# Other places for the quantization units, and split weights kept in DRAM for the second batch

## The chip, the cores and the metric

The kernel runs on one core of one Trainium2 chip. The metric is the device time of one execution in microseconds (us); the median of three runs of the kernel before is 3158.2 us (3157.79 to 3158.3).

## The reference

One launch computes two transformer layers on x (2 batches x 512 rows x 1024), in float32:

```python
x = x + xattn(layernorm(x), ctx, ctx, mask, wq, wk, wv, wo)     # 32 query heads, 8 key/value heads, rotary, softmax
x = x + router(layernorm(x))    # softmax over 64 experts, top 8: flat * sum(w) + w @ expert_bias
x = x + fake_quant(layernorm(x)) @ fake_quant(ctx)              # 8-bit codes, product of codes
x = x + (silu(y @ dq1.T) * (y @ dq2.T)) @ dq3.T                 # y = layernorm(x); dq = nf4(w), hidden size 2752
```

nf4(w) quantizes each block of 64 weights: it divides by the block's largest magnitude, takes the nearest of 16 code values, and multiplies back. Context rows number 1024 per batch.

## The kernel before, in words

The program has three stages, one after the other, each with an instruction list per engine written out by hand as a loop over slots. An engine works in program order and waits on semaphores. Matrix products take each float32 operand as a high part (float32r) and a low part (the rest), and run three TensorE (PE) matmuls per tile: high by high, low by high, high by low (`split_matmul`, L130). So each operand needs a copy on ScalarE (ACT) for the high part and a subtraction on VectorE (DVE) or GpSimd (POOL) for the low one.

**Front** (`front_stage`): 128 tiles of 24 matmuls, keys (32), values (32 + 32 around the second batch's keys) and queries (64). ACT rounds a head's weights, POOL makes their low half two tiles ahead (L714), DVE and POOL rotate key and query tiles (L658, L659, L728, L731). **Attention** (`attention_stage`): 64 heads in 256 steps of scores, softmax, transposes and mixing. **Tail** (`tail_stage`): slots 0 to 127 project the heads on wo ("head" slots, 12 matmuls each, a ring of four heads loaded from DRAM, rounded by ACT at L1634, low half by DVE at L1736 or POOL at L1912); then the FFN. The router and the quantized product of each batch are a chain of small links, put into given slots by `Chain`: batch 0 in head slots 64 to 111, batch 1 in slots 128 to 175. Before it the 16 context tiles are turned into codes: ACT scales (L1639), POOL clips (L1916), DVE rounds to bfloat16 (L1751), SP stores.

**The FFN's items** (`Plan`): the hidden size is cut into 22 chunks. Items 0 to 7 take chunks 0 to 7 for batch 0 alone, while the chain of batch 1 runs; items 8 to 15 take the same eight chunks for batch 1; items 16 to 29 take chunks 8 to 21 for both batches. An item has two slots of 12 matmuls for each of its gates (gate and up, one or two batches); every second item also holds the "down" slots of the pair before. For every item the weights come from DRAM (`load_weight`, three loads of 512 KB), PE turns them in six turns of four transposes (`turn`, L2021), ACT copies the high part (`weight_high`) and DVE subtracts for the low part (`weight_low`) into the buffers `gu` and `dn`, which alternate by item.

**The nf4 units** (`Nf4`): the quantization of w1, w2 and w3 is cut into 65 units of 128 x 1024 weights, which fill DVE, ACT and POOL beside the other work. A unit has DVE's maximum by block (L212 and two short ones), POOL's normalization (L224), seven ramps on ACT (L241), each followed by a step on DVE (L262, then L265 six times), then a subtraction on DVE (L268), a sign (L245) and three folds (L250) on ACT, two last steps on DVE (L271, L273), and POOL's multiplication (L278); SP loads and stores it. `Spread` cuts a unit into 12 places and spreads these over slots by weights. The units are split 34 / 12 / 8 / 11 over front, attention, the head slots and the FFN from item 8 on. A unit of the FFN must be stored before `load_weight` of its chunk.

Of the kernel before, what the change touches and what calls it, by code (L numbers as in the profile page):

```python
# [26 lines left out]
P = 128  # L27
# [49 lines left out]
TINY = 1e-30  # L77
SIGNS = NP4 + len(FOLDS)
NS4 = NP4 + len(FOLDS) + 2
# [57 lines left out]
class Nf4:  # L137
# [89 lines left out]
    def above_scalar(self, act, n, s, steps, width=D):  # L227
# [3 lines left out]
        for j in steps:  # L231
            f = j - NP4 - 2
            if j < NP4:
# [9 lines left out]
            if f == 0:  # L243
                act.wait_ge(self.stepped.sem, n * ND4 + 2 * ND4 + NP4 + 1)
                act.activation(x, x, ACT.Sign, bias=self.sharp[:, SIGNS:SIGNS + 1]).then_inc(self.above_done.sem, 1)  # L245
            if f >= 0:
                scale, _, slope = FOLDS[f]
                if f:
                    act.wait_ge(self.above_done.sem, n * NA4 + NP4 + 1 + f)
                act.activation(fold, fold if f else self.val[:, s, w], ACT.Prelu, bias=self.sharp[:, NP4 + f:NP4 + f + 1],  # L250
                               scale=scale, alpha=slope).then_inc(self.above_done.sem, 1)
# [43 lines left out]
class Spread:  # L295
# [4 lines left out]
    def __init__(self, units, weights, lag=1, sync_lag=1, ahead=8):  # L300
        total = units * NS4
        edge, run, whole = [0], 0.0, float(sum(weights))
        for w in weights:
# [5 lines left out]
        self.steps, self.maxes, self.norms, self.finishes, self.loads, self.stores = (  # L309
            [[] for _ in range(slots)] for _ in range(6))  # L310
        where = {}
        for q in range(len(weights)):
            for k in range(edge[q], edge[q + 1]):
                self.steps[q].append(divmod(k, NS4))
                where[divmod(k, NS4)] = q
        for u in range(units):
            if u:
                assert where[u - 1, ahead] < where[u, 0] and (u < 2 or where[u - 2, NS4 - 1] < where[u - 1, ahead])
                self.maxes[where[u - 1, ahead]].append(u)
                self.norms[where[u - 1, ahead] + lag].append(u)  # L320
# [29 lines left out]
def front_stage(nc, ident, sharp, x, context, wq, wk, wv, tables, q_d, k_d, v_d, rows, units, handover):  # L350
# [4 lines left out]
    with ExitStack() as ctx:  # L355
# [132 lines left out]
        plan = Spread(len(units), [weight(kind, n) for kind, n, _ in ORDER])  # L488
# [140 lines left out]
        def _(dve):  # L629
# [44 lines left out]
            for q, (kind, n, half) in enumerate(ORDER):  # L674
# [28 lines left out]
                for u, j in plan.steps[q]:  # L703
                    nf.step_vector(dve, u, u % 2, [j], parts[u], units[u][2])
                    if j == 8 and u + 1 < len(units):
# [5 lines left out]
        def _(pool):  # L711
# [26 lines left out]
            for q in range(plan.slots):  # L738
                kind, n, half = ORDER[q] if q < len(ORDER) else ("end", 0, 0)
                if kind == "tile":  # L740
# [4 lines left out]
                    if n == 64:  # L745
                        pool.wait_ge(tab_q, 32)
                for u in plan.norms[q]:
                    nf.norm_gpsimd(pool, u, u % 2, units[u][2])
                for u in plan.finishes[q]:
                    nf.finish_gpsimd(pool, u, u % 2, units[u][2])  # L750
# [70 lines left out]
def attention_stage(nc, q_d, k_d, v_d, r_d, o_d, mask, ident, ho, old, sharp, units):  # L821
# [8 lines left out]
    with ExitStack() as ctx:  # L830
# [84 lines left out]
        plan = Spread(len(units), [n >= UNITS_FROM for n in range(ALL - 4)], lag=2, sync_lag=6)  # L915
# [181 lines left out]
        def _(dve):  # L1097
# [27 lines left out]
            def do_step(n):  # L1125
# [9 lines left out]
                for u, j in planned(plan.steps, n - 1):  # L1135
                    nf.step_vector(dve, u, u % 2, [j], u // 2)
                    if j == 8 and u + 1 < len(units):
# [61 lines left out]
class Plan:  # L1199
# [8 lines left out]
    def __init__(self):  # L1208
        self.slots = [("head", q // HQ, q % HQ) for q in range(self.FIRST)]
        self.turn_no, self.turn_slot, self.turns = {}, {}, {}  # L1210
        self.gate_no, self.a_no, self.h_until = {}, {}, {}
# [18 lines left out]

    def _turn(self, i, x, q):
        if i < self.NI:
# [940 lines left out]
```

## Time and profile before

| | us |
|---|---|
| median of 3 runs | 3158.2 |
| the profiled execution | 3158.93 |
| its span, first to last instruction | 3157.2 |
| PE busy in the span | 2954.9 (94%) |
| DVE busy | 2311.9 (73%) |
| ACT busy | 1919.0 (61%) |
| POOL busy | 1094.0 (35%) |

The front lasts to about 845 us, attention to 1812, the head slots to 2287; items 0 to 7 of the FFN end at 2497, items 8 to 15 at 2639. Busy times are sums over instructions; matmuls are pipelined and their ends modelled, so a busy PE is not PE at its peak. The granted clock of TensorE is 1.00 at full speed.

### The profile page before, as it was taken

How to read it: one execution, taken by the hardware profiler on the slowest of the kernel's cores; microseconds unless marked ns; L12 is line 12 of the kernel's file. 1: busy time of each engine (PE TensorE's matmuls, PEld its weight loads, DVE VectorE, ACT ScalarE, POOL GpSimd, SP SyncE). 2: the span in 40 equal slices, each digit the busy share in tenths (PEclk: the TensorE clock that was granted, in tenths of full speed). 3: DMA queues.
4: the chain of work that ended last, by engine and by line, in shares of the span. 5: the costliest groups of instructions: out<-in, count | busy, mean ns of one | idle time of the engine just before them, and what ended most of it. 6: DMA issues, size and time to landing. Idle time of an engine off the chain costs nothing. (4 is left out here: it accounts for less than half of the span.)

```text
span 3157.2 us, 39853 instructions
## 1 busy us (share of the span) xinstructions
PE 2954.9 (94%) x14326; PEld 2414.3 (76%) x14336; DVE 2311.9 (73%) x3394; ACT 1919.0 (61%) x2643; POOL 1094.0 (35%) x644
## 2 busy tenths in 40 slices
PE   7989899989799999999999978998999999999999
PEld 6767687767588888888888856776786788888887
DVE  5878788788588888888888748788456666666633
ACT  4676666666488888888888756655343344444411
POOL 4626428777623333333333246543300000000000
PEclk9999999999899999999999989999999999999999
DMA  5445344343332222222222187743421232222111
GB/s 181 143 151 169 120 136 134 114 137 127 125 109 83 79 94 84 78 94 81 88 101 73 55 301 261 242 166 132 169 67 61 85 96 87 74 72 67 60 37 57
DMA packets 231108, 362.18 MB, mean 115 GB/s; under 512 B 19456, under 2 KB 114688, under 8 KB 230912
## 3 DMA queue, kind: packets, MB, share of 16 engines
q1 hardware_dynamic: 230912, 359.63, 34.4%
q8 instruction: 115, 1.88, 0.2%
q14 instruction: 81, 0.66, 0.1%
HBM read 266.90 MB, written 92.67 MB: 114 GB/s over the span
## 5 line engine op out<-in xcount | busy, mean ns | idle before, releaser
L1108 DVE CUSTOM_DVE_ANT_0 at_sc<-at_s,at_mk 128x1024 f32<-128x1024 f32 x256 | 312.0, 1219 | 100.6 <-issue 98.2
L132 PE MATMUL fr_acc<-fr_xh,fr_wh 128*128 128x512 f32 x768 | 308.8, 402 | 57.6 <-POOL fr_wl L714 52.4
L241 ACT ACTIVATE fr_nf_above<-fr_nf_raw,sharp 128x1024 f32<-128x1024 f32 (+1 forms) x238 | 258.8, 1103 | 164.6 <-POOL fr_nf_raw L224 107.0
L1123 DVE TENSOR_TENSOR at_ptl<-at_t,at_pth 128x512 fp32r<-128x512 f32 x512 | 326.5, 679 | 30.6 <-ACT at_pth L1070 30.6
L1070 ACT ACTIVATE at_pth<-at_t 128x512 fp32r<-128x512 f32 x512 | 277.4, 595 | 112.0 <-PE at_t L1170 111.3
L1060 ACT ACTIVATE at_pr<-at_sc,at_low 128x1024 f32<-128x1024 f32 x256 | 295.7, 1155 | 36.0 <-DVE at_low L1108 30.6
L133 PE MATMUL fr_acc<-fr_xl,fr_wh 128*128 128x512 f32 x768 | 305.4, 398 | 0.0
L134 PE MATMUL fr_acc<-fr_xh,fr_wl 128*128 128x512 f32 x768 | 305.0, 397 | 0.0
L1170 PE MATMUL at_t<-ident,at_pr 128*128 128x128 f32 x2048 | 267.8, 273 | 12.2 <-DVE at_ptl L1123 11.2
L1170 PEld LDWEIGHTS at_t<-ident,at_pr 128*128 128x128 f32 x2048 | 236.3, 140 | 53.9 <-issue 19.3
L265 DVE SCALAR_TENSOR_TENSOR fr_nf_val<-fr_nf_above,fr_nf_val 128x1024 f32<-128x1024 f32 (+1 forms) x204 | 246.5, 1209 | 20.4 <-ACT fr_nf_above L241 3.2
L132 PE MATMUL tl_pa<-tl_ring_h 128*128 128x512 f32 x512 | 210.0, 410 | 40.9 <-POOL tl_ring_l L1912 16.1
L1912 POOL TENSOR_TENSOR tl_ring_l<-tl_ring,tl_ring_h 128x1024 fp32r<-128x1024 f32 x64 | 162.5, 2539 | 193.6 <-ACT tl_ring_h L1634 193.5
L132 PEld LDWEIGHTS fr_acc<-fr_xh,fr_wh 128*128 128x128 f32 x768 | 148.4, 193 | 99.3 <-issue 58.0
L132 PE MATMUL at_o<-at_pth,at_vh 128*128 128x512 f32 x512 | 221.9, 433 | 0.2 <-DVE at_ptl L1123 0.2
L132 PE MATMUL at_s<-at_kh,at_qh 128*128 128x512 f32 x512 | 201.8, 394 | 11.8 <-POOL at_ql L1004 11.8
L1652 ACT ACTIVATE tl_gu<-tl_pt 128x512 fp32r<-128x512 f32 x120 | 71.7, 597 | 226.5 <-PE tl_pt L2021 226.5
L1764 DVE TENSOR_TENSOR tl_gu<-tl_pt,tl_gu 128x512 fp32r<-128x512 f32 x120 | 82.6, 688 | 169.8 <-ACT tl_gu L1652 169.2
L133 PE MATMUL tl_pa<-tl_ring_l,tl_ring_h 128*128 128x512 f32 x512 | 203.9, 398 | 0.0
L134 PE MATMUL tl_pa<-tl_ring_h,tl_ring_l 128*128 128x512 f32 x512 | 203.6, 398 | 0.0
L134 PE MATMUL at_s<-at_kh,at_ql 128*128 128x512 f32 x512 | 201.9, 394 | 0.0
L134 PE MATMUL at_o<-at_pth,at_vl 128*128 128x512 f32 x512 | 201.1, 393 | 0.0
(224 smaller groups left out, 7842.6 us busy)
## 6 DMA issues: line engine op xcount, KB each, us to landing
tl_raw<-dq SPq DMA_DIRECT2D x87, 512.0 KB, 3.6
tl_ring<-o_d SPq DMA_DIRECT2D x128, 256.0 KB, 3.2
tl_ring<-in_L_xattn_wo SPq DMA_DIRECT2D x128, 256.0 KB, 3.9
fr_nf_raw<-in_L_ffn_w SPq DMA_DIRECT2D x33, 512.0 KB, 3.6
dq<-fr_nf_val SPq DMA_DIRECT2D x33, 512.0 KB, 3.6
fr_raw<-in_L_xattn_wq SPq DMA_DIRECT2D x32, 512.0 KB, 4.5
q_d<-fr_res SPq DMA_DIRECT2D x64, 256.0 KB, 2.3
rows<-q_d SPq DMA_DIRECT2D x64, 256.0 KB, 2.7
```

The source lines that it names most:

```text
L132: pe.matmul(out, w[0], x[0], start=start, stop=False)
L133: pe.matmul(out, w[0], x[1], start=False, stop=False)
L134: return pe.matmul(out, w[1], x[0], start=False, stop=stop)
L241: act.activation(self.ramps[j % 2][:, w], x, ACT.Relu, bias=self.sharp[:, j:j + 1], scale=SHARP).then_inc(self.above_done.sem, 1)
L265: dve.scalar_tensor_tensor(v, above, STEPS[j], v, ALU.min, ALU.add).then_inc(self.stepped.sem, 1)
L1060: act.activation(pr[:, n % 2], sc[:, n % 2], ACT.Exp, bias=low[:, n % 2:n % 2 + 1], scale=-1.0, accum_out=sums[:, h % 2, quarter:quarter + ...
L1070: act.activation(pt[0][:, h % 2, j * HALF:(j + 1) * HALF, (n % QT) * P:(n % QT + 1) * P], t_ps[:, j], ACT.Copy).then_inc(t_hi.sem, 1)
L1108: dve.tensor_tensor_reduce(sc[:, n % 2], s_ps[:, n % 2], mk[:, bb * QT + n % QT], -1.0, -NEG, ALU.add, ALU.min, low[:, n % 2:n % 2 + 1]).t ...
L1123: dve.tensor_tensor(pt[1][sl], t_ps[:, j], f32(pt[0][sl]), ALU.subtract).then_inc(t_lo.sem, 1)
L1170: last = pe.transpose(t_ps[:, j, c, :], pr[:, n % 2, k * P:(k + 1) * P], ident[:])
L1764: dve.tensor_tensor(lo, pt[:, no % 2], f32(hi), ALU.subtract).then_inc(w_lo, 1)
L1912: pool.tensor_tensor(ring_l[:, q % 4], ring[:, q % 4], f32(ring_h[:, q % 4]), ALU.subtract).then_inc(ring_lo_p, 1)
```

## The change

- The units are split 28 / 12 / 6 / 19 (`chunks, late_units` from 12, 8 to 9, 6).
- Within a unit the folds come before the sign and do not wait for the subtraction; a unit has 11 places instead of 12. DVE takes a unit's step when ACT is at the next one (`late`), in the front and the tail. The next unit's maximum stands at place 5 (before: 8, in the tail 7). POOL takes finishes before normalizations. In the front SP loads and stores a unit one slot later. In the FFN a "down" slot has 0.3 of the weight of a gate slot.
- The context codes: ACT scales, rounds and codes (three passes), POOL clips between; DVE has no part. They begin at slot 5 instead of 3, and each tile is stored four slots after its scaling instead of two.
- DVE waits for the router's inputs at slot 62 instead of before its first low half; SP loads them at slot 40; the scales' loads, the first context tiles, and the loads of x come later and spread.
- In the chain, codes and product come one slot later, and the last normalization and turn too.
- Items 0 to 7 store their split weights to DRAM (`keep`, 24 stores of 1 MB on SP's queue). Items 8 to 15 load no raw weights and have no turns, copies or subtractions; POOL's queue loads the split weights back (`fetch`, 24 loads of 1 MB), and PE waits for these.

The core of the diff:

```diff
+AHEAD = 5
-NS4 = NP4 + len(FOLDS) + 2
+NS4 = NP4 + len(FOLDS) + 1
@@ Nf4.above_scalar
-            f = j - NP4 - 2
-            if j < NP4:
+            f = j - NP4
+            if f < 0:
...
+            elif f < len(FOLDS):
+                scale, _, slope = FOLDS[f]
+                if f:
+                    act.wait_ge(self.above_done.sem, n * NA4 + NP4 + f)
+                else:
+                    act.wait_ge(self.stepped.sem, n * ND4 + 2 * ND4 + NP4)
+                act.activation(fold, fold if f else self.val[:, s, w], ACT.Prelu, ...
+            else:
                 act.wait_ge(self.stepped.sem, n * ND4 + 2 * ND4 + NP4 + 1)
                 act.activation(x, x, ACT.Sign, bias=self.sharp[:, SIGNS:SIGNS + 1]).then_inc(self.above_done.sem, 1)
@@ Spread
                 where[divmod(k, NS4)] = q
+                if k:
+                    self.late[q].append(divmod(k - 1, NS4))
@@ front_stage
-        plan = Spread(len(units), [weight(kind, n) for kind, n, _ in ORDER])
+        plan = Spread(len(units), [weight(kind, n) for kind, n, _ in ORDER], lag=1, sync_lag=2)
...
-                for u, j in plan.steps[q]:
+                for u, j in plan.late[q]:
@@ Plan
+    def again(self, i):
+        return self.EARLY <= i < 2 * self.EARLY
     def _turn(self, i, x, q):
-        if i < self.NI:
+        if i < self.NI and not self.again(i):
@@ Plan._item
+        self.item_slot[i] = len(self.slots)
+        for j in range(2):
+            self._fetch(i + 1, j, self.item_slot[i] + 1)
+        self._fetch(i, 2, self.item_slot[i] + (1 if i % 2 else len(mine) - 2))
@@ Chain._batch
-        r, z, y = [6 + 3 * t for t in range(QT)], [27 + 3 * t for t in range(QT)], [43 + t for t in range(QT)]
+        r, z, y = [6 + 3 * t for t in range(QT)], [27 + 3 * t for t in range(QT)], [44 + t for t in range(QT)]
...
-                put("pe", z[t] + 2, "product", t, h)
+                put("pe", z[t] + 3, "product", t, h)
@@ tail_stage, SP
+            def keep(i, j):
+                sp.wait_ge(w_lo, plan.turn_no[i, 2 * j + 3 if j < 2 else 1] + 1)
+                sp.dma_start(split_d[i, j], f32(parts_of(i, j))).then_inc(kept[j][i % 2], 16)
...
+                for i, xx in plan.turns.get(q - 2, []):
+                    if xx in (1, 3, 5) and i < plan.EARLY:
+                        keep(i, {3: 0, 5: 1, 1: 2}[xx])
@@ tail_stage, ACT
+            def round_context(n):
+                act.wait_ge(ones_made, 1)
+                act.wait_ge(ctx_scaled, n + 1)
+                act.activation(rows[:, n % 2], rows[:, n % 2], ACT.Identity, bias=rounding[:, 0:1]).then_inc(ctx_rounded, 1)
+            def code_context(n):
+                act.wait_ge(ctx_clipped, n + 1)
...
+                if 2 <= i < plan.EARLY:
+                    act.wait_ge(kept[(xx - 2) // 2 if xx >= 2 else 2][i % 2], 16 * (i // 2))
@@ tail_stage, DVE
-            dve.wait_ge(ro_in, 48)
             low(1)
             for q in range(TOTAL + 2):
+                if q == plan.BASE[0] - 2:
+                    dve.wait_ge(ro_in, 48)
@@ tail_stage, POOL
+            def fetch(i, j):
+                pool.wait_ge(kept[j][i % 2], 16 * max((i - plan.EARLY) // 2 + 1, min(i, plan.EARLY) // 2))
+                if j < 2:
+                    pool.wait_ge(gated, plan.gate_no[i - 2, plan.halves(i - 2)[-1], 1] + 1)
+                else:
+                    pool.wait_ge(y_tiles, plan.y_base[i // 2])
+                pool.dma_start(parts_of(i, j), split_d[i - plan.EARLY, j]).then_inc(fetched[j][i % 2], 16)
@@ tail_stage, PE
+                    if plan.again(i):
+                        pe.wait_ge(fetched[u][i % 2], 16 * ((i - plan.EARLY) // 2 + 1))
+                    else:
+                        pe.wait_ge(w_lo, plan.turn_no[i, 2 * u + 3] + 1)
@@ build
-    chunks, late_units = 12, 8
+    chunks, late_units = 9, 6
```

## Rows read from the trace of the kernel before

**Rows 1.** Windows by stage: length, PE, PEld, DVE, ACT, POOL busy; clock; DMA; GB/s.

```profile
0.00:500.00 500.00, 439.25 (x1950) 359.04 (x1951) 386.01 (x429) 325.90 (x370) 246.95 (x162) 0.97 0.46 149
500.00:845.00 345.00, 307.17 (x1286) 247.97 (x1285) 272.25 (x290) 216.00 (x238) 259.76 (x163) 0.96 0.38 123
845.00:1812.00 967.00, 942.80 (x5147) 792.20 (x5147) 809.54 (x1572) 794.76 (x1318) 309.75 (x190) 0.99 0.26 88
1812.00:2007.00 195.00, 155.95 (x649) 124.02 (x647) 126.60 (x106) 117.80 (x115) 109.42 (x52) 0.91 0.80 276
2007.00:2287.00 280.00, 260.61 (x1187) 201.06 (x1192) 212.49 (x263) 149.30 (x167) 119.09 (x50) 0.97 0.49 166
2287.00:2497.30 210.30, 198.74 (x1020) 155.01 (x1025) 132.71 (x252) 73.68 (x118) 4.18 (x4) 0.98 0.21 63
2497.30:2639.20 141.90, 141.87 (x710) 117.17 (x709) 91.69 (x126) 65.94 (x91) 11.44 (x6) 1.00 0.34 104
2639.20:3157.20 518.00, 508.55 (x2387) 417.81 (x2385) 280.65 (x362) 175.68 (x228) 33.37 (x19) 1.00 0.20 62
```

**Rows 2.** Waits of PE, 0 to 845 us: total, times, longest.

```profile
PE fr_acc L132 <- POOL fr_wl L714: 52.4, 21, 7.3
PE fr_acc L764 <- DVE rows L670: 15.1, 1, 15.1
```

**Rows 3.** Timeline of PE around one turn (start, length, instruction).

```profile
2468.16 0.39 PE L134 MATMUL tl_pa<-tl_yT,tl_gu 128*128 128x512 f32 x1
2468.39 0.60 PE L2021 MATMUL tl_pt<-ident,tl_raw 128*128 128x128 f32 x4
...
2469.06 0.39 PE L133 MATMUL tl_pa<-tl_yT,tl_gu 128*128 128x512 f32 x1
...
2471.34 0.39 PE L134 MATMUL tl_pa<-tl_yT,tl_gu 128*128 128x512 f32 x1
```

**Rows 4.** DVE's groups, 500 to 845 us: busy, mean ns, idle before.

```profile
L265 DVE SCALAR_TENSOR_TENSOR fr_nf_val<-fr_nf_above,fr_nf_val 128x1024 f32<-128x1024 f32 x78 | 95.6, 1225 | 6.5
L658 DVE TENSOR_TENSOR fr_tb<-fr_acc,fr_sin 64x512 f32<-64x512 f32 x53 | 36.7, 693 | 6.5 <-ACT fr_res L608 5.0
...
L262 DVE TENSOR_SCALAR fr_nf_val<-fr_nf_above 128x1024 f32<-128x1024 f32 x13 | 15.9, 1225 | 41.2 <-ACT fr_nf_above L241 41.1
```

**Rows 5.** POOL's groups, 500 to 845 us.

```profile
L731 POOL TENSOR_TENSOR fr_res<-fr_res,fr_tb 128x512 f32<-128x512 f32 x54 | 73.6, 1362 | 46.7 <-DVE fr_tb L659 45.8
...
L278 POOL TENSOR_TENSOR fr_nf_val<-fr_nf_val,fr_nf_am 128x1024 f32<-128x1024 f32 x13 | 24.8, 1910 | 0.0
```

**Rows 6.** DMA issues: KB each, median us to landing.

```profile
tl_ring<-in_L_xattn_wo SPq DMA_DIRECT2D x128, 256.0 KB, 3.9
...
tl_qb<-qb_d SPq DMA_DIRECT2D x2, 2048.0 KB, 9.7
...
at_mk<-in_mask_BxSxS_ff SPq DMA_DIRECT2D x1, 2048.0 KB, 13.2
```

**Rows 7.** The chain of waits, 1820 to 1845 us: start, length, what.

```profile
1826.72 13.47 DMA tl_two<-in_L_ffn_router_bias
```

**Rows 8.** Timeline of PE at the tail's start, idle time in brackets.

```profile
1825.11 0.80 PE L132 MATMUL tl_pa<-tl_ring_h 128*128 128x512 f32 x1 [12.18 <-POOL tl_ring_l L1912]
...
1841.56 0.79 PE L132 MATMUL tl_pa<-tl_ring_h 128*128 128x512 f32 x1 [11.27 <-DVE tl_ring_l L1736]
```

**Rows 9.** DVE's groups, 1840 to 2040 us.

```profile
L1751 DVE TENSOR_SCALAR tl_codes<-tl_rows 128x1024 bf16<-128x1024 f32 x16 | 27.0, 1686 | 6.7 <-POOL tl_rows L1916 6.7
...
L262 DVE TENSOR_SCALAR tl_nf<-tl_above 128x1024 f32<-128x1024 f32 x5 | 11.7, 2331 | 0.0
```

**Rows 10.** ACT's groups, 1840 to 2040 us.

```profile
L1634 ACT ACTIVATE tl_ring_h<-tl_ring 128x1024 fp32r<-128x1024 f32 x63 | 65.9, 1051 | 38.0 <-DMA tl_ring<-in_L_xattn_wo 20.4 <-PE tl_pa L134 17.3
...
L1639 ACT ACTIVATE tl_rows<-tl_rows,tl_two 128x1024 f32<-128x1024 f32 x16 | 19.7, 1230 | 0.0
```

**Rows 11.** Waits of PE, 2007 to 2287 us.

```profile
PE tl_pc L2060 <- DVE tl_two L1846: 8.6, 3, 4.2
```

More of the change, by code:

```diff
@@ L295, with __init__ @@
 class Spread:
-    def __init__(self, units, weights, lag=1, sync_lag=1, ahead=8):
+    def __init__(self, units, weights, lag=1, sync_lag=1, ahead=AHEAD, norm_lag=1):
         total = units * NS4
@@ L308, in __init__ @@
         self.units, self.slots = units, slots
-        self.steps, self.maxes, self.norms, self.finishes, self.loads, self.stores = (
-            [[] for _ in range(slots)] for _ in range(6))
+        self.steps, self.late, self.maxes, self.norms, self.finishes, self.loads, self.stores = (
+            [[] for _ in range(slots)] for _ in range(7))
         where = {}
@@ L315, in __init__ @@
                 where[divmod(k, NS4)] = q
+                if k:
+                    self.late[q].append(divmod(k - 1, NS4))
+        self.late[where[divmod(total - 1, NS4)] + 1].append(divmod(total - 1, NS4))
         for u in range(units):
@@ L319, in __init__ @@
                 self.maxes[where[u - 1, ahead]].append(u)
-                self.norms[where[u - 1, ahead] + lag].append(u)
+                self.norms[where[u - 1, ahead] + norm_lag].append(u)
             end = where[u, NS4 - 1]
@@ L914, in attention_stage @@
         nf = Nf4(tools, sharp)
-        plan = Spread(len(units), [n >= UNITS_FROM for n in range(ALL - 4)], lag=2, sync_lag=6)
+        plan = Spread(len(units), [n >= UNITS_FROM for n in range(ALL - 4)], lag=2, sync_lag=6, norm_lag=2)
         def planned(table, n):
@@ L1136, in do_step @@
                     nf.step_vector(dve, u, u % 2, [j], u // 2)
-                    if j == 8 and u + 1 < len(units):
+                    if j == AHEAD and u + 1 < len(units):
                         nf.max_vector(dve, u + 1, (u + 1) % 2, (u + 1) // 2)
@@ L1371, in due, with tail_stage @@
         return self.at[engine].get(q, [])
-def tail_stage(nc, o_d, wo, x, context, scales, router_w, router_b, expert_b, dq, dq3, qb_d, ident, ident_bf, sharp,
+def tail_stage(nc, o_d, wo, x, context, scales, router_w, router_b, expert_b, dq, dq3, qb_d, split_d, ident, ident_bf, sharp,
                o_units, f_units, chunk_unit, out):
@@ L1465, in tail_stage @@
         raw_in = [sem(f"raw_in{j}") for j in range(3)]
+        kept, fetched = [[[sem(f"{n}{j}{s}") for s in range(2)] for j in range(3)] for n in ("kept", "fetched")]
         zeroed, out_stored = sem("zeroed"), sem("out_stored")
@@ L1640, in scale_context @@
                                scale=kq[:, 1:2]).then_inc(ctx_scaled, 1)
+            def round_context(n):
[4 more added lines that the diff above has]
+                act.wait_ge(ctx_clipped, n + 1)
+                if n >= 2:
+                    act.wait_ge(ctx_out[n % 2], 16 * (n // 2))
+                act.activation(codes[:, n % 2], rows[:, n % 2], ACT.Identity, bias=rounding[:, 1:2]).then_inc(ctx_coded, 1)
             def weight_high(i, xx):
```

155 lines of the change are left out of this document (87 added, 68 removed).

## The prediction

> **What bounds the kernel now.** I read the busy time by stage first, then TensorE's (PE's) waits stage by stage, then the rows of the engine it waits for. Most stages are TensorE's own: attention (845 to 1812 us) has PE busy 942.8 of 967 us, the FFN from item 8 on 141.87 of 141.9 and 508.55 of 518 [rows 1]. PE loses time in two places. In the front (0 to 845) it is idle 500 - 439.25 = 60.8 and 345 - 307.17 = 37.8 us, and mean clocks of 0.97 and 0.96 cost about 0.03 x 439 + 0.04 x 307 = 25 us more [rows 1]. In the tail's projection (1812 to 2287) it is idle 39.0 and 19.4 us [rows 1]. In the front the largest wait is for POOL's low half of a head's weights, 52.4 us in 21 times; the largest single one is 15.1 us for DVE's normalized row [rows 2]. Both engines work in program order, so either wait is the lag of a queue filled with quantization units. In the query part (500 to 845) DVE handled 53 rotated tiles, 6.5 us each, where 24 matmuls at 0.228 us need 5.47 (ten spacings from 2469.06 to 2471.34 [rows 3]). DVE was busy 272.25 us [rows 1]; the rotations take 53 x 2 x 0.693 = 73 [rows 4], so the units take 199, or 14.7 each (78 whole L265 steps, 6 to a unit, and half a unit: 13.5 units). It also waited 41.2 us at L262 [rows 4], which makes 91% before smaller waits. POOL was busy 259.76 of 345 us [rows 1].
>
> **The change, part by part.** The sum is made against the profiled execution (3158.93 us, span 3157.2, so 1.7 us outside the span); the median shown is 3158.2, 0.7 lower, and I take the sum off the median.
>
> *Units 34/12/8/11 to 28/12/6/19.* Six units leave the front, two leave the projection, and eight join the FFN. In the query part DVE drops to 199 x 28/34 = 164 + 73 = 237 us per 53 tiles, 4.5 us a tile against 5.47; POOL loses 6/34 of its unit time (13.5 units x 2 x 1.91 = 52 us [rows 5]), 260 to 251, or 4.7 a tile. Both then fit under PE. Also, DVE now takes a step when ScalarE (ACT) is already at the next one, so the wait at L262 should mostly go; the subtraction and first fold no longer wait for each other; and a unit has 11 places instead of 12. What is late next is POOL: 2 x 1.36 us of its 4.7 are rotations [rows 5], and it waits for DVE's last step at each unit. The load of the next raw unit is issued one slot later as well, nearer to its reduction. I take 5.85 us a tile, between 5.47 and 6.5: 64 tiles x 0.65 = 42 us. Before 500 us I take 14 of the idle time, most of the 15.1 us wait. Front: -56; bounds -20 (POOL merely takes DVE's place) and -100 (all but the start-up's share of the 124 lost).
>
> *Eight more units in the FFN.* 8 x 14.7 = 118 us of DVE, beside PE. From 2639 us on DVE is busy 280.65 of 518 and ACT 175.68 [rows 1]. By the planner 1.57 unit steps fall on each gate slot in place of about 0.8, which is 1.57 x 14.7/11 = 2.1 us of a 2.73 us slot; with products, low halves and additions an item of 12 slots needs some 31 us of DVE under 35 of PE. Each unit still has 8 or more slots between its store and its use. I take +5 for adds that come late (a down tile needs the addition two tiles before); bounds 0 and +27, which is 7% of the 390 us in which units run, if DVE waits as it did in the front.
>
> *Kept weights.* For items 8 to 15, 8 x 6 = 48 turns of four transposes go from PE, with 48 copies on ACT and 48 subtractions on DVE, both off PE's path. A turn costs PE 0.444 us: from the matmul at 2468.16 to the second one after the turn, at 2469.06, is 0.90, where two plain spacings are 0.456 [rows 3]. 48 x 0.444 = 21.3. As a check: 528 matmuls x 0.228 = 120.4 us, and the stage takes 141.9 [rows 1]. All of it is on the path: -21. It adds 24 stores of 1 MB on SP's queue in items 0 to 7, each behind the loads of raw weights and ahead of the unit stores. SP waits there for DVE's low half; queued behind are the next raw loads, needed an item later. 24 MB over 210 us is 114 GB/s on top of 63, under the 276 that the projection carries for 195 us [rows 1]; ACT's copy two items later waits for a store that had an item's time. Cost 0; up to +15 if ACT stands at it, since the gates' activations queue behind. It also adds 24 loads of 1 MB on POOL's queue. Each waits for the gates of the item two before; behind it on POOL stand the clip, the unit's finish and its normalization, with slots to spare. No POOL-issued DMA is in this trace. The nearest rows are SP's: 2 MB landed in 9.7 and in 13.2 us [rows 6], so 4.9 to 6.6 per MB. An even item after an odd one gives 4 x 2.73 = 10.9 us for its first MB, so a load at either rate lands in time. With 1 MB for each of six units the traffic is 30 MB in some 125 us, 240 GB/s, also under 276. I take 0 (nearest the 9.7 us row, which is a load into SBUF amid other traffic); bounds 0 and 24 x 6.6 = 158 us against 120: +38.
>
> *Start of the tail.* DVE's first low half no longer waits for the router's bias: that transfer is 13.47 us of the chain [rows 7], and PE waited 11.27 us for the low half at 1841.56 [rows 8]. Next late are the ring's own loads. -12, with part of what the 0.91 mean clock of that stretch costs [rows 1]; bounds -8 and -15.
>
> *Context codes on ACT.* DVE loses 16 x 1.686 = 27.0 us [rows 9]. ACT gets two more passes for each of 16 tiles, one tile in 3 slots: 3 x 1.05 + 3 x 1.23 [rows 10] + 3 x 0.68 unit steps of about 1.1 = 9.1 us per 3 slots, where PE needs 8.2. So ACT bounds slots 5 to 53, at 16 x 0.9 = 14 us over PE. But PE now has 39.0 - 12.2 (before its first matmul [rows 8]) - 11.3 = 15.5 us of waits left in that stretch, mostly DVE's lag; one takes the other's place. 0; bounds -12 and +15. The loads of X, now spread, and scales later: 0, they relieve a queue at 276 GB/s.
>
> *Chain one slot later.* Codes, products and the last turn move by a slot. PE's 8.6 us of waits for L1846 [rows 11] and part of the other 11 idle us in that stretch go, with DVE lighter by a quarter of its units: -12; bounds -3 and -20. In items 0 to 7 the same gains about 3 and loses about 3: the last turn now stands right before the first gate of item 8, and its copy and subtraction must pass. 0.
>
> Sum: -56 + 5 - 21 - 12 + 0 - 12 + 0 = -96, so 3158.2 - 96 = 3062.
>
> **The rivals.** *POOL or DVE stays the bound* (23%): the front gains 20 instead of 56 and the FFN loses 15 instead of 5: 3062 + 36 + 10 = 3108. For it: POOL's 4.7 us a tile and its order; against: its 46.7 us of idle time at L731 [rows 5], nearly all of it for DVE. *The front becomes PE's* (10%): -95 in place of -56, 3023. For it: DVE falls to 82% of a tile.
>
> *The kept weights come too late from POOL's queue, slower than before* (6%): PE stands in items 8 to 15 for 24 loads. Decided at (120 + 96)/24 = 9.0 us per MB; above that the gain is spent. At four times a single 256 KB load's 3.9 us [rows 6], 15.6 per MB if POOL's queue carried only one small piece at a time, items 8 to 15 would take 374 us: 3062 + 254 = 3316. Against it: the 2 MB rows. For it: the rows show DVE and POOL holding each other up. The same kind of L262 takes 1.225 us in the front [rows 4] and 2.331 in the projection [rows 9], where POOL reads much of the time.
> The Trainium skill ("SBUF — State Buffer", section "SBUF: two separate sides") states that a DMA issued from GpSimd gets its descriptors from GpSimd's own cores, and that these are shut out while VectorE runs an instruction that takes their shared port pair, so that the transfer looks blocked. By that rule a load would start up to one such instruction late, 2.3 us by the row; three even items have 10.9 - 6.6 = 4.3 us to spare, so it costs nothing here unless it strikes many times in one load. The rows agree on the contention; none shows it on a DMA.
>
> *Nothing measurable* (4%): the front's gain missing and the FFN's DVE cost at its bound: -21 - 12 - 12 + 27 + 15 = -3.
>
> **How the numbers follow.** The forecast case, 3035 to 3095, has 57%. Low end 3015: the PE-bound front (3023) with some of the context stretch's -12. High end 3130: the POOL-bound case with 22 of the +38 for late loads. Runs of the kernel before differ by 0.5 us, so 0.2%, 6.3 us, is about what can be told from no change. Faster 57 + 23 + 10 = 90%, same 4%, slower 6%.
>
> **What would show it.** Front: the wait for L714's half falls from 52 to under 25 us, and attention begins near 790 to 800. Tail start: no wait of 11 us before the second head. Items 8 to 15: no transposes, and 120 to 125 us from the first gate to item 16; a wait of PE for a DMA into the weights there means the loads are late. FFN: DVE at about 85% of the stretch with units, PE above 97%. Wrong would be a front above 835 us, PE waits over 20 us in items 8 to 15, or a projection stretch longer than now.

## The result, and the profile after

The changed kernel takes 3132.5 us (median of 4 runs, 3126.09 to 3139.28) against 3158.25: 0.9912 of the time before, 95% interval 0.9900 to 0.9923, a gain of 26 us where 96 were forecast. Its profiled execution is the fastest of its four: 3126.09 us, 32.8 under that of before. The stages below sum to this number.

The windows by stage of the changed kernel (columns as in [rows 1]; the front now ends at 754 us, attention at 1729):

```profile
0.00:500.00 500.00, 476.47 (x2155) 394.48 (x2156) 379.28 (x423) 315.02 (x365) 275.79 (x180) 0.99 0.47 154
500.00:753.90 253.90, 252.58 (x1111) 207.65 (x1109) 199.99 (x222) 156.72 (x177) 216.47 (x137) 1.00 0.42 134
753.90:1728.90 975.00, 938.66 (x5121) 786.26 (x5120) 813.26 (x1567) 795.65 (x1317) 309.10 (x185) 0.99 0.26 87
1728.90:1918.50 189.60, 157.75 (x644) 126.10 (x645) 93.06 (x77) 138.37 (x137) 104.90 (x53) 0.91 0.77 267
1918.50:2206.00 287.50, 263.29 (x1193) 201.71 (x1191) 205.54 (x249) 137.26 (x155) 113.30 (x48) 0.96 0.51 173
2206.00:2413.60 207.60, 194.20 (x997) 150.58 (x997) 129.24 (x247) 70.09 (x112) 7.26 (x8) 0.99 0.52 188
2413.60:2549.50 135.90, 128.19 (x545) 104.43 (x545) 95.49 (x105) 65.94 (x69) 35.44 (x30) 0.95 0.57 197
2549.50:3121.00 571.50, 526.45 (x2387) 427.34 (x2384) 366.63 (x443) 247.91 (x297) 63.27 (x32) 0.97 0.20 66
```

PE is now busy 252.6 of 253.9 us in the query part: that part of the front is now limited by PE alone. In the last window PE is idle 45 us at a mean clock of 0.97, where it was idle 9.5 at 1.00 [rows 1].

For a comparison by stage I take the starts of fixed matmuls in the timelines of PE: the first score matmul and the last output matmul of attention, the first matmuls of head slots 5 and 53, and the first gates of items 0 (slot 128), 8, 16 and 27 (the 2nd column is a start, the others are lengths, in us).

| kernel | first score | attention | to slot 5 | slots 5-53 | slots 53-128 | items 0-7 | items 8-15 | items 16-26 |
|---|---|---|---|---|---|---|---|---|
| before | 863.5 | 949.0 | 42.6 | 152.3 | 279.7 | 210.2 | 141.9 | 396.7 |
| after | 765.0 | 963.5 | 28.0 | 162.1 | 287.5 | 207.5 | 135.9 | 453.6 |
| difference | -98.5 | +14.5 | -14.6 | +9.8 | +7.8 | -2.7 | -6.0 | +56.9 |

From item 27 on both kernels take 114.5 us to the start of the last tile. (The expectations below say "items 16 to 29" for the last column.) So the front alone gave what was forecast for the whole, and 89 us were lost again behind it: 14.5 in attention, 17.6 in the head slots and 57 in the FFN. Items 8 to 15 gained 6 where the kept weights were to give 21.

How far can such lengths be read? Among the profiled executions below, a stage that runs the same code still varies: the front by 5 us, attention by 5, slots 53 to 128 by 7, items 0 to 7 by 4, items 8 to 15 by 3, and slots 5 to 53 and items 16 to 26 by under 1. The changed kernel's 287.5 and 207.5 us in slots 53 to 128 and items 0 to 7 are at the short end of this; its 135.9 us in items 8 to 15 is the longest (132.6 and 132.8 in two other kernels with that code).

The 57 us of items 16 to 26 are not idle time alone. PE is idle 43.2 us there, against 4.2 before, and its busy time for the same matmuls grew from 392.5 to 410.4 us, at a mean granted clock of 0.96 against 1.00. So about 39 us are waits and 18 go with the lower clock.

PE's waits in the changed kernel (total, times, longest), first in the front, then from slot 128 to the end; and for items 16 to 26 alone, before and after:

```profile
PE fr_acc L770 <- DMA rows<-in_ctx: 9.1, 3, 6.5
PE fr_acc L133 <- POOL fr_wl L720: 5.9, 3, 4.6
...
PE fr_acc L770 <- DVE rows L676: 3.0, 2, 2.6
```

```profile
PE tl_pa L133 <- DVE tl_X L1834: 44.6, 16, 6.6
```

```profile
PE tl_pa L132 <- DVE tl_X L1776: 4.2, 5, 1.3
```

```profile
PE tl_pa L133 <- DVE tl_X L1834: 34.9, 11, 6.6
```

The 52.4 us for POOL's low half and the 15.1 us for the row [rows 2] are nearly gone from the front. DVE's rotations and POOL's, 500 to 754 us (busy, mean ns, idle before):

```profile
L664 DVE TENSOR_TENSOR fr_tb<-fr_acc,fr_sin 64x512 f32<-64x512 f32 x47 | 32.6, 693 | 42.2 <-ACT fr_res L614 41.9
```

```profile
L737 POOL TENSOR_TENSOR fr_res<-fr_res,fr_tb 128x512 f32<-128x512 f32 x47 | 65.7, 1397 | 11.7 <-DVE fr_tb L665 9.5
```

DVE, which had waited 41.2 us inside its units [rows 4], now waits 42.2 at the rotations, for ACT's copy of the next tile, while PE is idle 1.3 us in all: DVE no longer holds PE up there. POOL's wait for DVE, 45.8 us before [rows 5], is 9.5. In the FFN one wait has come up: a "down" matmul stands until DVE has added the tile that holds its PSUM buffer. DVE's timeline ahead of one such wait, and PE's and POOL's there (start, length, instruction, idle time before):

```profile
2628.66 1.22 DVE L268 SCALAR_TENSOR_TENSOR tl_two<-tl_two 128x1024 f32<-128x1024 f32 x1
2629.80 1.21 DVE L213 TENSOR_REDUCE tl_am<-tl_two 128x16 f32<-128x1024 f32 x1
...
2631.68 2.88 DVE L268 SCALAR_TENSOR_TENSOR tl_two<-tl_two 128x1024 f32<-128x1024 f32 x1 [0.18 <-issue]
2634.60 1.23 DVE L271 TENSOR_TENSOR tl_two<-tl_two 128x1024 f32<-128x1024 f32 x1
2635.74 1.28 DVE L1834 TENSOR_TENSOR tl_X<-tl_pa,tl_X 128x512 f32<-128x512 f32 x2
```

```profile
2636.48 0.80 PE L133 MATMUL tl_pa<-tl_dn,tl_hT 128*128 128x512 f32 x1 [5.45 <-DVE tl_X L1834]
```

```profile
2631.59 1.90 POOL L225 TENSOR_TENSOR tl_two<-tl_two,tl_am 128x1024 f32<-128x1024 f32 x1 [11.96 <-DVE tl_am L220]
```

For 7 us DVE does nothing but unit work: a step, the next unit's maximum, a step that takes 2.88 us instead of 1.22 while POOL normalizes beside it, and a subtraction. The addition that PE needs is queued behind. DVE is not full (325.2 of the 453.5 us of items 16 to 26); its work comes in lumps. In the longest wait, 6.6 us, DVE itself stands idle first, for ACT's sign (L254), with the addition behind the unit's last steps:

```profile
2960.18 1.23 DVE L274 SCALAR_TENSOR_TENSOR tl_two<-tl_two 128x1024 f32<-128x1024 f32 x1 [3.36 <-ACT tl_two L254]
2961.44 1.22 DVE L276 TENSOR_TENSOR tl_two<-tl_two 128x1024 f32<-128x1024 f32 x1
2962.58 1.28 DVE L1834 TENSOR_TENSOR tl_X<-tl_pa,tl_X 128x512 f32<-128x512 f32 x2
```

```profile
2963.32 0.80 PE L133 MATMUL tl_pa<-tl_dn,tl_hT 128*128 128x512 f32 x1 [6.60 <-DVE tl_X L1834]
```

ACT's waits in items 16 to 26, by the line of the waiting instruction (L242 a ramp, L250 the first fold, L268 DVE's step, L276 its last one):

```profile
ACT tl_two L250 <- DVE tl_two L268: 59.5, 15, 7.1
ACT tl_two L242 <- DVE tl_two L268: 44.8, 32, 6.0
ACT tl_two L242 <- DVE tl_two L276: 31.9, 10, 10.3
```

The same tie shows in the head slots, 5 to 88, where ACT also has the two new passes. There ACT, held at the first fold, takes a ring head's high half late, and POOL's low half (L1972) and PE's head follow it:

```profile
ACT tl_pt L250 <- DVE tl_nf L268: 23.7, 5, 8.5
```

```profile
PE tl_pa L133 <- POOL tl_ring_l L1972: 14.9, 6, 3.9
PE tl_pc L2125 <- DVE tl_two L1875: 7.4, 1, 7.4
```

(The second fence is PE's from 1860 to 2206 us.) POOL has a tie of its own there. Its normalization of the next unit (L225) now stands for DVE's maximum of the same slot, 36.9 us in all from slot 5 to 128, where it stood 0.4 in the kernel before, and the next head's low half is queued behind it. Four of PE's nine waits for POOL's low half in these slots (2.7 to 3.9 us each) follow such a normalization directly. One of them, POOL's rows and PE's:

```profile
2037.89 2.75 POOL L225 TENSOR_TENSOR tl_nf<-tl_nf,tl_am 128x1024 f32<-128x1024 f32 x1 [15.51 <-DVE tl_am L220]
2040.61 5.67 POOL L1972 TENSOR_TENSOR tl_ring_l<-tl_ring,tl_ring_h 128x1024 fp32r<-128x1024 f32 x2
```

```profile
2043.99 0.50 PE L133 MATMUL tl_pa<-tl_ring_h 128*128 128x512 f32 x1 [3.89 <-POOL tl_ring_l L1972]
```

No run below moves that normalization by itself. The weights kept in DRAM came back in time. DMA issues (KB each, median us to landing) and PE's wait for one, in items 8 to 15:

```profile
tl_gu<-split_d POOLq DMA_DIRECT2D x16, 1024.0 KB, 7.3
...
tl_dn<-split_d POOLq DMA_DIRECT2D x8, 1024.0 KB, 7.0
```

```profile
PE tl_pc L133 <- DMA tl_gu<-split_d: 2.7, 1, 2.7
```

### The profile page after: what moved, and what is told of

It reads as the page before. It is cut to its first block and busy times, and to the rows that moved or that the text cites. A ratio compares the mean times of both kernels' runs of the same rounds, so it can differ in the third digit from the quotient of the medians.

```text
span 3124.3 us, 39400 instructions
## 1 busy us (share of the span) xinstructions
PE 2937.6 (94%) x14144; PEld 2398.6 (77%) x14144; DVE 2282.7 (73%) x3330; ACT 1926.9 (62%) x2627; POOL 1125.5 (36%) x670
## 5 line engine op out<-in xcount | busy, mean ns | idle before, releaser
L1114 DVE CUSTOM_DVE_ANT_0 at_sc<-at_s,at_mk 128x1024 f32<-128x1024 f32 x256 | 311.9, 1219 | 105.5 <-issue 104.3
L133 PE MATMUL fr_acc<-fr_xh,fr_wh 128*128 128x512 f32 x768 | 300.2, 391 | 7.6 <-POOL fr_wl L720 5.9
L242 ACT ACTIVATE fr_nf_above<-fr_nf_raw,sharp 128x1024 f32<-128x1024 f32 (+1 forms) x196 | 215.8, 1102 | 112.5 <-DVE fr_nf_val L268 52.3
L242 ACT ACTIVATE tl_two<-tl_two,sharp 128x1024 f32<-128x1024 f32 x133 | 152.5, 1148 | 118.2 <-DVE tl_two L268 56.4
L1972 POOL TENSOR_TENSOR tl_ring_l<-tl_ring,tl_ring_h 128x1024 fp32r<-128x1024 f32 x64 | 158.8, 2482 | 174.4 <-ACT tl_ring_h L1681 174.4
L268 DVE SCALAR_TENSOR_TENSOR fr_nf_val<-fr_nf_above,fr_nf_val 128x1024 f32<-128x1024 f32 (+1 forms) x168 | 201.3, 1198 | 13.7 <-ACT fr_nf_above L242 3.0
L1800 DVE TENSOR_TENSOR tl_ring_l<-tl_ring,tl_ring_h 128x1024 fp32r<-128x1024 f32 x64 | 99.0, 1547 | 151.6 <-ACT tl_ring_h L1681 151.5
L1015 POOL TENSOR_TENSOR at_ot<-at_ot,at_inv_row 128x512 f32<-128x512 f32 x64 | 85.2, 1331 | 323.1 <-ACT at_ot L1082 323.1
```

Of the source, the lines that this page charges most:

```text
L133: pe.matmul(out, w[0], x[0], start=start, stop=False)
L242: act.activation(self.ramps[j % 2][:, w], x, ACT.Relu, bias=self.sharp[:, j:j + 1], scale=SHARP).then_inc(self.above_done.sem, 1)
L268: dve.scalar_tensor_tensor(v, above, STEPS[j], v, ALU.min, ALU.add).then_inc(self.stepped.sem, 1)
L1114: dve.tensor_tensor_reduce(sc[:, n % 2], s_ps[:, n % 2], mk[:, bb * QT + n % QT], -1.0, -NEG, ALU.add, ALU.min, low[:, n % 2:n % 2 + 1]).t ...
L1800: dve.tensor_tensor(ring_l[:, q % 4], ring[:, q % 4], f32(ring_h[:, q % 4]), ALU.subtract).then_inc(ring_lo_d, 1)
L1972: pool.tensor_tensor(ring_l[:, q % 4], ring[:, q % 4], f32(ring_h[:, q % 4]), ALU.subtract).then_inc(ring_lo_p, 1)
```

## The experiments

Theory: the change gains in the front by six units fewer and loses behind it because DVE and ACT, each in program order, get unit work in lumps and in step with each other, so that the products' own work on them comes late. Rivals: the kept weights or the stores crowd the FFN; the units' number alone costs, whatever their order; the moved context passes cost. Each time is a median, of four or more executions but for the even spread, which has two; the kernel before took 3157 to 3159 us beside them.

**Units as before.**

```diff
-    chunks, late_units = 9, 6
+    chunks, late_units = 12, 8
```

> The changed kernel with the units split 34/12/8/11 again; all else as changed. Theory A (the number of units in a stage sets its time): from item 16 on 518 to 522 us in place of 574.8, items 8 to 15 about 122 to 126 in place of 135.9, and the front back up from 765 to 800 to 815 us; in sum about 3095. Rival B (the order of the steps and DVE's step one slot later made the front's gain, not the six units fewer): the front stays at 765 to 775, in sum about 3060. Rival C (the FFN's loss is not the units but the kept weights' traffic): from item 16 on stays at 560 or more.

3186.65 us, 1.0085 [1.007, 1.010] of before: with the old split 34/12/8/11 the rest of the change makes the kernel slower, which none of the theories had foreseen. By stage: first score at 862.5 us, attention 965.4, to slot 5 27.8, slots 5 to 53 180.0, 53 to 128 297.8, items 0 to 7 210.7, items 8 to 15 122.1, items 16 to 26 396.2. This one run separates most terms. At the old split the rest of the change gains 1 us in the front, which is within what the front varies; taking six units away then gives 97.5. What the old order would give with 28 units in the front was not run, so the split of the gain between the two holds in this order of edits only. At equal units the new order costs attention 16 us, and the order, the context passes and the later chain together cost the head slots 46 (27.7 + 18.1). Two units fewer take 17.9 and 10.3 us of that off again in the changed kernel. The kept weights give 19.8 us in items 8 to 15, and items 16 to 26 are at the length of before with 11 units. Against it the changed kernel's FFN is 13.8 + 57.4 = 71 us longer: the price of eight units more.

**Nothing kept.** Items 8 to 15 load, turn and split their weights again.

```diff
     def again(self, i):
-        return self.EARLY <= i < 2 * self.EARLY
+        return False
```

> The changed kernel without the kept weights: items 8 to 15 load raw weights and turn, copy and subtract again; nothing stored or fetched. Theory A (the 48 turns cost PE 21 us, and the 48 low halves burden a DVE that already comes late there): items 8 to 15 take 155 to 165 us in place of 135.9, total 20 to 30 us longer than the changed kernel. Rival (the fetches only trade turns for waits): items 8 to 15 136 to 142, total within 8 us. Second rival (late in items 16 to 29 is caused by the change of items 8 to 15): from item 16 on differs by over 10 us from 574.8.

3152.24 us, 0.9973 [0.9962, 0.9985]: 20 us above the changed kernel. Items 8 to 15 take 160.1 us against 135.9, items 16 to 26 450.5 against 453.6. So keeping gives 24 us where it acts, and the FFN's loss is there without the stores and loads: the rival that they crowd it falls.

**Even spread in the FFN.**

```diff
-            return 1.0 if s[0] == "gate" else 0.3
+            return 1.0
```

> The changed kernel with equal weights for gate and down slots in the FFN, so 1.3 unit steps a slot everywhere in place of 1.57 in gate slots and 0.47 in down slots. If two steps in one slot, which tie ACT's second step to DVE's first of the same slot, make DVE late: from item 16 on 540 to 555 us in place of 574.8. If what counts is DVE's time in the down slots, where the additions stand: 585 to 600. If only the number of units counts: 565 to 585.

3109.45 us, 0.9838 [0.9819, 0.9858]: 23 us below the changed kernel. Items 16 to 26 take 428.5 us. The same units on more slots cost 25 less, so their number alone isn't it.

**Unit steps first in the FFN.** In a slot DVE takes its unit steps ahead of the low halves that wait for ACT's copies.

```diff
+                for u, j in of2(spread2.late, q):
+                    nf2.step_vector(dve, u, u % 2, [j], parts2[u])
...
                 for i, xx in plan.turns.get(q - 1, []):
                     weight_low(i, xx)
...
-                for u, j in of2(spread2.late, q):
-                    nf2.step_vector(dve, u, u % 2, [j], parts2[u])
```

> The changed kernel, but in the FFN DVE takes a slot's unit steps ahead of the slot's low halves of weights and hidden values, behind products and additions as before. Nothing is added or left out. If the loss from item 16 on comes from the chain DVE step, ACT step, ACT copy, DVE low half within one slot (each waiting for the other while neither is full), it shrinks: 530 to 550 us in place of 574.8, and ACT's waits for L268 fall by half. If DVE simply has too much work: 565 to 585.

3107.96 us, 0.9836 [0.9821, 0.9850]: 24 us below. Items 16 to 26 take 432.7 us with the same work on each engine; only the order on DVE differs. One sign that was expected did not come: ACT's waits for DVE's steps (L268), which were to fall by half, fell from 104.3 to 88.8 us. What fell is DVE's own wait for ACT's copies at the weights' low halves, from 62.3 to 20.3 us: with the unit steps ahead of them, DVE no longer stands there with steps queued behind.

**Both.**

> Two edits together that each gave 24 us: unit steps spread evenly over all slots of the FFN instead of 1.0 on gate slots and 0.3 on the others, and VectorE's unit steps ahead of its low halves in a slot. Theory A (two separate losses: bunching of steps, and steps queued behind waits for ScalarE): items 16 to 29, 453.6 us in the changed kernel and 428.5 and 432.7 with one edit each, fall to about 410, and the time to about 3090. Rival B (one loss, ScalarE and VectorE waiting for each other in turn, of which either edit takes the same part): 425 to 430 us, and a time of about 3105.

3093.24 us, 0.9794 [0.9780, 0.9809], and items 16 to 26 417.3: of the two losses of 25 and 21 us 36 come back together, so they are mostly separate. Items 16 to 26 in these runs (us; PE's longest wait for an addition, and ACT's total wait for DVE at the first fold):

| kernel | length | PE busy | PE idle | clock | longest for an addition | ACT at the first fold |
|---|---|---|---|---|---|---|
| before | 396.7 | 392.5 | 4.2 | 1.00 | 1.3 | - |
| units as before | 396.2 | 393.2 | 3.0 | 1.00 | 2.0 | 44.3 |
| changed | 453.6 | 410.4 | 43.2 | 0.96 | 6.6 | 59.5 |
| even spread | 428.5 | 402.0 | 26.5 | 0.98 | 3.3 | 66.8 |
| steps first | 432.7 | 402.9 | 29.8 | 0.98 | 2.3 | 50.2 |
| both | 417.3 | 399.3 | 18.0 | 0.99 | 2.6 | 52.6 |

PE's idle time goes with the length; ACT's wait at the first fold does not. So the late additions are the cost, and what the tie at the first fold adds to them in the FFN is not shown.

**Two units back to the front, on top of both** (`chunks` 10 instead of 9: 30/12/6/17).

> As the run with both edits in the FFN, but with two units moved from the FFN back to the front: 30 units in the front, 12 in attention, 6 in the projection, 17 in the FFN. Theory A (the front is TensorE's from about 30 units down, and the FFN's loss grows with its units): the front stays within 10 us of its 765, items 16 to 29 lose another 5 to 10 us, and the time is level with the run with both edits or a few us below. Rival B (each unit in the front costs the same, 98 us for six): the front is 33 us longer, and the time 25 us above that run.

3099.17 us, 0.9814 [0.9798, 0.9830], 6 us above the run with both (their executions overlap: 3095.7 to 3106.8 and 3090.1 to 3099.5). The first score comes at 789.7 us against 766.7: 11.5 us a unit, and (862.5 - 789.7)/4 = 18.2 for each of the next four. The FFN gains 5.0 in items 8 to 15 and 10.9 behind. Rival B came nearer on the front, A on the FFN: neither is free at this split, and a unit costs more in the front (11.5) than in the FFN (8).

**Context codes back on DVE.** POOL's clip and SP's store of a context tile go back to their old slots with them (cut from the diff).

```diff
 act:
-                    if q == context_slot(n) + 1:
-                        round_context(n)
-                    if q == context_slot(n) + 3:
-                        code_context(n)
 dve:
+                for n in range(NC):
+                    if q == context_slot(n) + 1:
+                        round_context(n)
```

> Only the context codes go back: one rounding pass on VectorE in place of two passes on ScalarE, as in the kernel before; all else as in the changed kernel. Theory A (ScalarE sets the pace of slots 5 to 53 in the changed kernel): that stretch falls from 162.1 to about 150 us, the 152.3 of the kernel before with two units fewer, and the time falls by about 12 us. Rival B (the stretch is slow because the units' steps reach VectorE and GpSimd later, whatever ScalarE does): VectorE gets 27 us of work back, and the stretch stays at 160 to 170 us.

3123.15 us, 0.9888 [0.9872, 0.9903]. Slots 5 to 53 take 155.4 us: 6.7 of the 12 that A expected. The passes on ACT, with the later clip and store, cost something, but are not all of the loss there.

**The reduction on a fold's place, in attention.**

```diff
-... lag=2, sync_lag=6, norm_lag=2)
+... lag=2, sync_lag=6, ahead=8, norm_lag=2)
-                    if j == AHEAD and u + 1 < len(units):
+                    if j == 8 and u + 1 < len(units):
```

> In attention alone the reduction of the next unit goes from the place of step 5 to place 8, where VectorE has no step (the unit is then with ScalarE's folds); all else as in the changed kernel. Attention, from its first score matmul to its last output matmul, took 949 us in the kernel before and 963.4 in the changed one, at the same 12 units. Theory A (a reduction of 1.2 us on top of a step of 1.3 us in one slot makes VectorE's low halves late): attention falls back to about 950 us, TensorE's waits for the low halves from 23.9 to about 11 us, and the time falls by 13. Rival B (the new order of folds and sign costs it, whatever the place of the reduction): attention stays at 960 to 965 us.

3121.46 us, 0.9884 [0.9868, 0.9901]. Attention takes 953.3 us, 10 to 15 less than in the runs with the maximum at place 5. PE's waits for DVE's low half in attention, in the kernel before, in the changed kernel, then in this one:

```profile
PE at_t L1170 <- DVE at_ptl L1123: 11.2, 12, 1.6
```

```profile
PE at_t L1176 <- DVE at_ptl L1129: 23.9, 23, 2.4
```

```profile
PE at_t L1176 <- DVE at_ptl L1129: 13.8, 15, 1.8
```

At place 8 DVE has no step, at place 5 it has: most of attention's loss is this move, which the prediction did not price.

**A place of rest before the first fold.**

```diff
-NS4 = NP4 + len(FOLDS) + 1
+NS4 = NP4 + len(FOLDS) + 2
-            f = j - NP4
+            f = j - NP4 - 1
```

> Only a place of rest goes between ScalarE's seventh ramp and its first fold in every unit (12 places to a unit again, the sign still behind the folds); all else as in the changed kernel. Theory A (in the changed order the first fold needs VectorE's last step in the very slot in which VectorE takes it, so ScalarE stands there with the next head's high half or the weights' copies behind it): ScalarE's waits for VectorE's steps at the first fold, 12 us in slots 5 to 53, 11.7 in 53 to 88 and 59.5 in items 16 to 29, fall below a third; slots 5 to 88 lose 8 to 15 us, items 16 to 29 lose 10 to 20, and the time falls by 20 to 30 us from the changed kernel's 3132. Rival B (what counts is how many unit operations fall in one slot, and 12 places to a unit make that 9% more): no stage gains over 3 us, items 16 to 29 grow by 10 or more, and the time is 3132 or above.

3125.57 us, 0.9893 [0.9880, 0.9907]. Slots 5 to 53 take 154.4 us and 53 to 128 282.0: 13 us less together, as A has it, and the wait at the first fold (23.7 us in the changed kernel) no longer is among ACT's larger ones there. But items 16 to 26 take 461.1, 7.5 more, which is B's direction: there ACT still waits 51.8 us in 11 times at the first fold, and the rest only makes 12 places of 11 in the same slots. Attention, at 966.7, gains nothing by it. The time fell by 7 us where A had 20 to 30.

**The four edits that helped** (even spread, steps first, context codes on DVE, the reduction at place 8 in attention).

> The four edits that helped, together: even spread and steps first in the FFN, context codes on VectorE, the reduction on a fold's place in attention. Theory A (each acts in its own stage: -39, -9 and -11 us from the changed kernel's 3132): 3073 us, with each stage within 3 us of what it was with its own edit. Rival B (a stage that comes earlier or later shifts what the next one starts with, so the gains do not add): 3085 us or more.

3064.11 us, 0.9701 [0.9687, 0.9714]: 9 below what A had. Attention 952.7, slots 5 to 53 153.0, items 16 to 26 414.2: each stage is about where its own edit had put it.

**With the place of rest as well.**

> The four edits together and the place of rest as well. Theory A (the first fold's wait for VectorE is a loss of its own): 15 to 25 us below the run with the four edits. Rival B (places per slot decide): level with it or above.

3049.52 us, 0.9657 [0.9643, 0.9670]: 14.6 below, just short of A's range. Slots 5 to 128 fall from 442.6 to 423.4; items 16 to 26 grow from 414.2 to 423.9.

**Two units from the projection to the FFN** (the four edits, without the rest, `late_units` 4).

> The four edits together, and two units moved from the projection to the FFN: 28 in the front, 12 in attention, 4 in the projection, 21 in the FFN. Theory A (a unit costs about 14 us in the projection, where 8 in place of 6 took 28 us more, and about 8 us in the FFN, where 19 in place of 17 took 16): slots 5 to 128 lose 20 to 28 us, items 8 to 29 grow by 16, and the time is 5 to 12 us below the run with the four edits. Rival B (the FFN's loss grows faster than its units, as VectorE fills up): items 8 to 29 grow by 30 or more, and the time is above.

3067.51 us, 0.9709 [0.9694, 0.9724], level with the four edits. Slots 5 to 128 take 19.6 us less, items 8 to 26 20.0 more and items 0 to 7 3.4 more: by then a unit costs 10 to 12 us in either place, and the FFN's price has grown from 8.

**The rest everywhere but in the FFN.**

> As the run with the four edits and the place of rest, but with no place of rest in the FFN's units (11 places there, 12 elsewhere). Theory A (in the projection the first fold's wait holds up the heads behind it on ScalarE; in the FFN the loss goes by how many unit operations fall in a slot): slots 5 to 128 keep their 423 us, items 8 to 29 go from 554.9 back to the 545 of the four edits, and the time falls from 3049.5 to about 3040. Rival B (the 10 us of the FFN come from the state in which the projection leaves it, a unit earlier or later): items 8 to 29 stay at 552 to 558 and the time at 3047 to 3052.

3040.72 us (3040.63 to 3041.74), 0.9624 [0.9611, 0.9637], as A has it: slots 5 to 128 422.6 us, items 8 to 26 547.0 against 554.9. This kernel is the best of all, 118.6 us under the one before. Its windows of items 16 to 26 and 8 to 15, and slots 5 to 53:

```profile
2500.10:2917.70 417.60, 399.45 (x1851) 325.24 (x1850) 328.18 (x382) 231.38 (x267) 59.85 (x28) 0.99 0.25 77
2370.70:2500.10 129.40, 123.12 (x543) 100.17 (x544) 99.98 (x106) 67.83 (x72) 36.10 (x30) 1.00 0.61 207
1740.80:1882.40 141.60, 135.32 (x585) 109.59 (x584) 115.92 (x81) 100.63 (x99) 96.25 (x45) 0.98 0.87 305
```

DVE carries 328 us in items 16 to 26, as in the changed kernel (325), and the stretch is 36 us shorter. PE's wait for the additions there, against 34.9 us and 6.6 at the longest:

```profile
PE tl_pa L133 <- DVE tl_X L1839: 18.1, 12, 2.6
```

## Why the prediction was wrong

- **The step that failed is "Eight more units in the FFN": +5 forecast, bounds 0 and +27; +71 measured** (13.8 in items 8 to 15, 57.4 behind, against the run with the old split). Its working was an average: 31 us of DVE under 35 of PE in an item. That sum holds still (325.2 us in 132 slots, 29.6 in 12), and so does the amount: 108 us more DVE work in items 8 to 26 than with the old split, where 118 were forecast. What failed is the step from a share that fits to an overlap that costs nothing. It left out where the work lies: unit steps, the next unit's maximum and the subtraction come in runs on DVE, the steps queue behind low halves that wait for ACT, and the additions that free PE's buffers stand behind all of it. Shown by the runs with even spread and with steps first: the same units, 25 and 21 us less. Of the 57 us in items 16 to 26 about 39 are waits and 18 the lower clock after them, which had no term. The upper bound of +27 was 7% of 390 us by DVE's waits in the front; the 7% is not worked out there (41.2 of 345 us would be 12%), and those were DVE's waits, not PE's behind DVE. Not settled is the last part: 417 us in the run with both edits and in the best kernel against 397, with PE idle 18 us in place of 4; and the tie of DVE and ACT at the first fold is seen in the FFN, but its price there is not.
- **Units fewer in the front: -56 forecast, -98.5 measured.** The direction was right, the size that of the rival "the front becomes PE's" (-95). I kept POOL as the next bound; its waits fell from 52.4 to 5.9 us. The order and `late`, to which part of the gain was put down, give 1 us at the old split; with 28 units in the front they were not tried by themselves.
- **Attention: no term, +14.5.** Units there keep their number, and I took their new order to be free. The maximum now shares a slot with a step; moving it away gave 10 us back. The rest of 4 is no more than attention varies from run to run with the same code (5 us). The place of rest alone did not help there (966.7).
- **Kept weights: -21 forecast, -20 and -24 measured** (with 11 units and with 19). The mechanism and price are right, and the rival of late loads did not come about: one wait of 2.7 us. They are not seen in the changed kernel's 135.9 us because units took 14 of them.
- **Start of the tail: -12 forecast, -14.6 measured.** The 11.27 us wait [rows 8] is gone.
- **Context codes on ACT: 0 forecast (to +15), +9.8 measured**, with two units fewer in the projection; at equal units these slots are 27.7 us longer. Taking the passes back gives 6.7, the place of rest 7.7, both together 20.6 (162.1 to 141.5). That another wait would go in exchange was wrong: new waits came, for DVE's step at the first fold and for its maximum at POOL's normalization.
- **Chain one slot later: -12 forecast, +7.8 measured**, up to +14.6 in other kernels with the same code here, and +18.1 at equal units. PE's waits for L1846 [rows 11] did go, but one of 7.4 us at another link came, and heads of the ring came late, behind ACT's first fold and POOL's normalization. The place of rest took 5.5 us off it. The shift of the chain was not undone by itself, so its own share stays open.

Summed: -98.5 + 14.5 - 14.6 + 9.8 + 7.8 - 2.7 - 19.8 + 13.8 + 56.9 = -32.8, the difference of the two profiled executions. That the kernel came out faster at all was luck: the front gave 42 us more than forecast, which hid most of the 66 us that the FFN's term was short. Of the prediction's own signs of trouble a longer projection stretch was there: 477.6 us against 474.6 up to item 0, and 449.6 against 432.0 from slot 5. PE was to stay above 97% in the FFN; in items 16 to 26 it was busy 90%.

The Trainium skill ("SBUF — State Buffer", section "SBUF: two separate sides") has a GpSimd-issued DMA look blocked while VectorE runs an instruction in a mode that holds the port pair the two share. Here the 24 loads landed in 5.2 to 10.4 us, and the trace gives the slow ones another reason in the main: three issued in a row at 2466.8, 2467.5 and 2468.2 us landed after 5.6, 7.4 and 9.8 us, the first beside a DVE instruction of 2.8 us. Three that stood first took 7.7 to 8.7 us, and why stays open. So the stall is not shown, and PE's one wait of 2.7 us is all that it waited for the loads. For instructions the same section has an exclusive lock: whichever of a VectorE instruction with two SBUF inputs and a GpSimd one that reads SBUF starts first runs, and the other waits. The trace agrees: POOL's normalization began 0.09 us before the step of 2.88 us, and the step ended 1.07 us after it. It lies in front of a late addition, so it is part of that wait.

## What to carry to other kernels

Filler work on an engine that works in program order is not priced by its share of the engine's time alone: at 72% busy DVE still made PE wait, by the run of filler that stood in front of an instruction PE needed. Look at the slots where most of it meets, and at what is queued behind a wait for another engine. When two engines hand a unit back and forth, a step that needs the other's result of the same slot ties both queues; in this kernel a place of rest gave 13 us in the projection and cost 7.5 in the fuller slots of the FFN. When one edit moves work between stages, run the kernel with the old split first: here that one run gave the size of most terms. And a wait costs more than its length when the clock falls with it: compare the busy time of the same matmuls too.

## What the runs showed of the hardware

- 1 MB loads issued from POOL's queue landed in 7.0 to 7.3 us (median) beside SP's traffic, at 197 GB/s in that window, and each issue held POOL 0.6 to 0.7 us (median). I had estimated 4.9 to 6.6. The median mixes two cases: a load that stands first mostly landed in 5.2 to 5.6 us (ten of thirteen), a second and third issued right behind it in 7.2 to 10.4.
- The same step on DVE takes 1.22 us alone and 2.88 us beside a POOL normalization. The 2.331 us of L262 in [rows 9] is a mean of one at 0.68 us, alone, and four at 2.4 to 2.9 beside POOL; the 1.225 of [rows 4], with which the prediction compares it, reads a ramp that lies in PSUM, and those did not grow beside POOL.
- The same matmuls of items 16 to 26 kept PE busy 392.5 us at a mean granted clock of 1.00 (before, waits of up to 1.3 us) and 410.4 at 0.96 (after, waits of up to 6.6 us).
